# One gather in 48 of a two-layer graph kernel replaced by 128 single-row loads from SyncE and ScalarE

## The chip, the cores and the metric

The kernel runs on one core of one Trainium2 chip. The metric is device time in microseconds, from the first to the last instruction of one execution with what lies around it; lower is better. The kernel before took 4138.44 us, the median of three runs (4134.31 to 4139.52).

## The reference

Two rounds of message passing over a graph with 6250 nodes and 200000 edges (sorted by destination), 128 features each, all in float32. Cut to what matters:

```python
edge_index = jnp.stack([src, dst])
# layer 0
m = relu(concat([x[dst], x[src], edge_attr, u_edge]) @ W1.T + b1)
agg = segment_sum(m, dst, 6250)
x = layernorm(x + relu(concat([x, agg, u]) @ W2.T + b2))
# layer 1
h = relu(concat([x[src], x[dst], edge_attr]) @ msg_w1 + msg_b1)
agg = mean over incoming edges of (h @ msg_w2 + msg_b2)      # 0 where a node has none
x = layernorm(x + relu(concat([x, agg]) @ upd_w1 + upd_b1) @ upd_w2 + upd_b2)
```

## The kernel before

The product over a concatenation is split. Each layer first makes two tables in HBM with one row per node: `tabQ` (x times the weights of the source part, float32, 512 bytes a row) and `tabP` (the destination part with the bias, as three bfloat16 pieces). An edge's message is then relu(edge_attr·wc + tabP[dst] + tabQ[src]).

The program is a row of blocks, with all engines meeting between them: setup and tables of layer 0, `edges(0)`, `update(0)` (node update, layer norm, new `tabQ`), `between()` (new `tabP`), `edges(1)`, `update(1)`. The two `edges` blocks hold nearly all the time. Each works through NG = 391 groups of GE = 512 edges, a group being J = 4 tiles of P = 128 edges. For group g:

- SyncE (the queue SP) loads the edge attributes `ea` (1 MB for four groups, line 528, two buffers), the destination numbers `bc` (for eight groups, line 534) and, for every group, the 42 rows of `tabP` that can occur in it (`PB`, line 538). The address of these rows is read from SBUF into a register (`value_load`, line 537). Before it loads `PB` of group g, SyncE waits until TensorE has finished the products of group g-4 (line 536), so it works up to four groups ahead.
- GpSimd (POOL) gathers the `tabQ` rows of the 512 source nodes with four indirect DMAs of 128 rows (`gathers`, line 206) into a ring `Qr` of R_Q = 12 groups. For group g it waits until VectorE has used group g-12 (line 204). The first PF = R_Q - 2 = 10 groups are gathered ahead of the block: in layer 0 in the setup block (line 291), in layer 1 in `between()` (line 844).
- TensorE adds the edge product (line 615, eight passes for four float32 products) and the `tabP` part by a 0/1 matrix (line 619) into one of four PSUM banks, and raises `v_C`. The group's messages of two groups before are summed by destination with line 628 (and counted with line 631, layer 0 only).
- VectorE makes the 0/1 matrices (lines 570, 576, 582), adds the gathered rows to the PSUM bank (line 587, this raises `v_tt`), and adds a finished group's sums to the accumulator (line 598).
- ScalarE does nothing else in these blocks than wait for `v_tt` and apply the relu (line 557), which raises `v_rl` for TensorE.

Each engine runs its own list in order; what holds them together are these semaphores and the depths of the rings.

Of the kernel before, what the change touches and what calls it, by code (L numbers as in the profile page):

```python
# [12 lines left out]
N = 6250  # L13
# [22 lines left out]

R_EA, R_PB, R_BC, R_Q, R_ST, R_S, R_M, R_PT = 2, 4, 2, 12, 3, 6, 3, 4
LB = 8
R_C = 4
PF = R_Q - 2  # L40
NBIG = 11904

WALL = ("wq0", "wp0", "wc0", "wu0", "w2x", "w2a", "w2u", "wq1", "wp1", "wc1", "mwT", "uwx", "uwa", "uw2")
# [4 lines left out]
def build(nc, a, out):  # L48
    ctx = ExitStack()
    with ctx:  # L50
# [31 lines left out]
        Qr = sb("Qr", [P, R_Q * J * D])  # L82
        Q = Qr[:, :].rearrange("p (r j d) -> p r j d", r=R_Q, j=J)
        X = sb("X", [P, NB, D])
        XT = sb("XT", [P, NP])
# [42 lines left out]
        for l in range(2):  # L128
            v = {n: sems(f"{n}{l}_", r) for n, r in (("ea", 3), ("pb", R_PB), ("bc", R_BC), ("q", R_Q))}
            v.update((n, sem(f"{n}{l}")) for n in ("C", "st", "s", "cn", "tt", "rl", "A", "ag"))  # L130
            v.update((n, sem(f"{n}{l}")) for n in ("gg", "gsc"))
            es.append(v)
# [63 lines left out]
        def pieces_sync(e, l, p_lo):  # L196
            for c, (b, n) in enumerate(CH):
                e.wait_ge(p_lo, c + 1)
                e.dma_start(node_rows(tabP[l], c), P3[:, c % R_PT, 0:n, :]).then_inc(s_tabP[l][c % R_PT], 16)

        def gathers(e, l, g0, g1):
            for g in range(g0, g1):
                if g >= R_Q:
                    e.wait_ge(es[l]["tt"], g - R_Q + 1)
                for j in range(J):
                    e.indirect_dma_start(Q[:, g % R_Q, j, :], None, tabQ[l][:, :],  # L206
                                         bass.IndirectOffsetOnAxis(ap=srcE[:, g, j:j + 1], axis=0)).then_inc(es[l]["q"][g % R_Q], 16)

# [8 lines left out]
        RQB = 4  # L217
        VALID = E - (NG - 1) * GE
        VJ, VP = VALID // P, VALID % P

# [282 lines left out]
        def edges(l):  # L503
# [14 lines left out]
            with nc.Block() as block:  # L518
                @block.sync
                def _(e):  # L520
                    ok = e.value_load(flagI[0:1, 0:1], min_val=0, max_val=1)
                    with e.If(ok):
                        for g in range(NG):
                            if g % LQ == 0:
                                k = g // LQ
                                if k >= R_EA:
                                    e.wait_ge(v_C, LQ * (k - R_EA) + LQ)
                                e.dma_start(ea[:, k % R_EA, :], a["eaT"][k, :, :]).then_inc(v_ea[k % R_EA], 16)
                            if g % LB == 0:
                                k = g // LB  # L530
                                n = min(LB, NG - g)
                                if k >= R_BC:
                                    e.wait_ge(v_st, LB * (k - R_BC) + LB)
                                e.dma_start(bc[0:K, k % R_BC, 0:n * GE], a["dstR"][:, g * GE:(g + n) * GE].broadcast_to([K, n * GE])).then_inc(v_bc[k % R_BC], 16)
                            if g >= R_PB:
                                e.wait_ge(v_C, g - R_PB + 1)
                            base = e.value_load(baseI[0:1, g:g + 1], min_val=0, max_val=N - 1)
                            e.dma_start(PB[0:K, g % R_PB, :], tabP[l][bass.ds(base, W), :].rearrange("w (h d) -> (w h) d", d=D)).then_inc(v_pb[g % R_PB], 16)
                    with e.Else():
                        general_sync(e, l)  # L540
# [9 lines left out]
                @block.scalar  # L550
                def _(e):
                    ok = e.value_load(flagI[0:1, 0:1], min_val=0, max_val=1)
                    with e.If(ok):
                        for g in range(NG):
                            e.wait_ge(v_tt, g + 1)
                            m = M[:, g % R_M, :, :].rearrange("p j d -> p (j d)")
                            e.activation(m, m, ACT.Relu).then_inc(v_rl, 1)  # L557

                @block.vector
                def _(e):  # L560
                    ok = e.value_load(flagI[0:1, 0:1], min_val=0, max_val=1)
                    with e.If(ok):
                        for i in range(NG + 3):
# [14 lines left out]
                            if 0 <= g < NG:  # L578
# [4 lines left out]
                                e.wait_ge(v_C, g + 1)  # L583
                                e.wait_ge(v_q[g % R_Q], 64 * (g // R_Q + 1))
                                if g >= R_M:
                                    e.wait_ge(v_A, g - R_M + 1)
                                e.tensor_tensor(M[:, g % R_M, :, :].rearrange("p j d -> p (j d)"), bank[g % R_C][:, :],  # L587
                                                Q[:, g % R_Q, :, :].rearrange("p j d -> p (j d)"), ALU.add).then_inc(v_tt, 1)
                            if l == 1 and i % 16 == 15 and i // 16 < NC:
# [285 lines left out]
def laid_out(v):  # L875
    import numpy as _np

    def cut(m, b):
# [15 lines left out]
        "eaT": eap.reshape(NQ, LQ * GE, D).transpose(0, 2, 1),  # L894
        "srcL": srcp.astype(_np.int32).reshape(NGP, J, P).transpose(2, 0, 1).reshape(P, NGP * J),
        "dstL": dstp.astype(_np.int32).reshape(NGP, J, P).transpose(2, 0, 1).reshape(P, NGP * J),
        "dstR": dstp.astype(_np.int16).reshape(1, EP),
# [22 lines left out]
```

## Time and profile before

| | |
|---|---|
| runs | 4139.52, 4138.44, 4134.31 us |
| profiled execution | 4140.49 us, its span 4138.7 us |
| GpSimd busy | 2981.5 us (72%) |
| TensorE matmul busy | 3378.5 us (82%), granted clock 0.517 over the span |
| VectorE busy | 1671.5 us (40%) |
| ScalarE busy | 591.0 us (14%) |
| DMA | 569.11 MB, mean 138 GB/s |

An engine's busy time leaves out the time that its queue needs between two instructions, and for POOL it is the time to make the descriptors of a gather, not the time of the transfer. DMA issues on SyncE and ScalarE are not counted as busy; their durations are found in the rows of their line (SPq and ACTq are these two queues). Which engine bounds a block is read from who waits for whom in it.

### The profile page before, as it was taken

Reading aid. Unit: us, or ns where it says so; the run is one execution under the profiler, and the core shown is the slowest. Engines: PE = TensorE matmul, PEld = TensorE weight load, DVE = VectorE, ACT = ScalarE, POOL = GpSimd, SP = SyncE. Lnnn points to the kernel's source line nnn. Section 1 sums busy time; section 2 is a strip of 40 time slices with the busy share of each in tenths; the row PEclk is TensorE's granted clock in tenths of the full one; section 3 lists DMA queues with packets and bytes.
Section 4 is the critical chain, followed back from the end, with each engine's and each line's share of the span. In section 5 each row is a group of like instructions: output and inputs, shape, how many; then the busy total and the mean of one; then the engine's idle time right before and its main releaser. Section 6 shows DMA issues by size and latency. Waiting matters only on the chain. (4 is left out here: it accounts for less than half of the span.)

```text
span 4138.7 us, 53825 instructions
## 1 busy us (share of the span) xinstructions
PE 3378.5 (82%) x16906; PEld 3171.1 (77%) x16906; DVE 1671.5 (40%) x3965; ACT 591.0 (14%) x1005; POOL 2981.5 (72%) x3156
## 2 busy tenths in 40 slices
PE   6998788877888888788779878878788787887886
PEld 4998787777878778787759877777777777777773
DVE  4544444444444444444445443434333333333333
ACT  1111111111111111111321111111111111111113
POOL 4777777777777777777267777777777777777772
PEclk6555555555555555555755555555555555555556
DMA  6554444444444444444155444444444444444431
GB/s 227 167 162 130 140 131 145 143 133 140 131 140 142 139 140 131 140 135 143 53 159 172 140 142 140 131 139 130 140 143 138 140 131 140 132 148 141 131 118 34
DMA packets 286577, 569.11 MB, mean 138 GB/s; under 512 B 165416, under 2 KB 197523, under 8 KB 248976
## 3 DMA queue, kind: packets, MB, share of 16 engines
q1 hardware_dynamic: 185326, 357.82, 25.7%
q0 software_dynamic: 100096, 205.20, 18.6%
q8 instruction: 142, 2.33, 0.2%
q10 hardware_dynamic: 866, 2.56, 0.2%
q14 instruction: 147, 1.20, 0.1%
HBM read 545.86 MB, written 19.45 MB: 137 GB/s over the span
## 5 line engine op out<-in xcount | busy, mean ns | idle before, releaser
L206 POOL DMA_INDIRECT Qr<-tabQ,srcE x3128 | 2960.7, 947 | 1074.7 <-issue 969.1
L615 PE MATMUL bank<-wall,BIG 128*128 128x128 f32 x6256 | 1596.3, 436 | 35.0 <-DMA BIG<-in_eaT 35.0
L628 PE MATMUL bank<-BIG 128*128 128x42 f32 x6256 | 1459.8, 413 | 13.0 <-ACT BIG L557 13.0
L615 PEld LDWEIGHTS bank<-wall,BIG 128*128 128x128 f32 x6256 | 1419.2, 331 | 35.4 <-DMA BIG<-in_eaT 35.4
L628 PEld LDWEIGHTS bank<-BIG 128*128 128x128 f32 x6256 | 1420.7, 331 | 13.6 <-ACT BIG L557 13.6
L587 DVE TENSOR_TENSOR BIG<-bank,Qr 128x512 f32<-128x512 f32 x782 | 539.6, 690 | 2097.9 <-issue 1727.3
L619 PE MATMUL bank<-BIG 126*128 126x128 bf16 x3128 | 484.1, 310 | 648.4 <-DVE BIG L570 647.8
L557 ACT ACTIVATE BIG<-BIG 128x512 f32<-128x512 f32 x782 | 492.4, 630 | 3364.1 <-DVE BIG L587 3364.1
L619 PEld LDWEIGHTS bank<-BIG 126*128 126x128 bf16 x3128 | 339.3, 141 | 774.8 <-DVE BIG L570 748.1
L570 DVE TENSOR_TENSOR BIG<-bank,BIG 126x512 bf16<-126x512 f32 x782 | 534.2, 683 | 34.3 <-DMA BIG<-in_dstR 34.0
L576 DVE TENSOR_TENSOR BIG<-bank,relE 128x168 f32<-128x168 f32 x782 | 251.5, 322 | 0.0
L598 DVE TENSOR_TENSOR AC<-AC,bank 128x84 f32 (+1 forms) x782 | 171.0, 219 | 162.4 <-PE bank L631 40.4
L582 DVE TENSOR_REDUCE BIG<-BIG 128x42 bf16<-128x168 f32 x391 | 167.5, 428 | 0.0
L631 PEld LDWEIGHTS bank<-BIG,onesb 128*128 128x128 bf16 x391 | 113.1, 289 | 0.0
L631 PE MATMUL bank<-BIG,onesb 128*128 128x42 bf16 x391 | 93.6, 239 | 0.0
L164 PEld LDWEIGHTS bank<-wall,XT 128*128 128x128 f32 x196 | 42.9, 322 | 34.7 <-issue 34.7
L819 POOL TENSOR_SCALAR BIG<-AC 3x512 bf16<-3x512 f32 (+1 forms) x13 | 18.8, 1446 | 59.1 <-PE bank L704 49.8
L162 PE MATMUL bank<-c,ones 1*128 1x512 f32 (+1 forms) x52 | 48.8, 1036 | 5.0 <-PEq L664 3.4
L164 PE MATMUL bank<-wall,XT 128*128 128x128 f32 x196 | 50.5, 436 | 0.0
L190 DVE TENSOR_TENSOR bank<-bank,BIG 128x512 f32<-128x512 f32 (+1 forms) x26 | 17.4, 668 | 74.9 <-ACT BIG L180 74.9
L402 DVE RECIPROCAL AC<-AC 128x512 f32<-128x512 f32 (+1 forms) x13 | 41.0, 3156 | 0.0
L702 PE MATMUL bank<-BIG,mU 128*128 128x512 f32 (+1 forms) x26 | 20.1, 867 | 22.1 <-DVE BIG L733 22.1
(94 smaller groups left out, 481.0 us busy)
## 6 DMA issues: line engine op xcount, KB each, us to landing
BIG<-in_eaT SPq DMA_DIRECT2D x196, 1024.0 KB, 5.6
BIG<-in_dstR SPq DMA_DIRECT2D x96, 1008.0 KB
Qr<-tabQ,srcE POOLq DMA_INDIRECT x3128, 2.5
BIG<-tabP SPq DMA_DIRECT2D x782, 31.5 KB
tabP<-BIG SPq DMA_DIRECT2D x24, 384.0 KB, 2.8
tabQ<-BIG SPq DMA_DIRECT2D x24, 256.0 KB, 4.0
X<-in_xN SPq DMA_DIRECT2D x1, 3136.0 KB, 12.0
out<-BIG SPq DMA_DIRECT2D x12, 256.0 KB, 2.3
```

What stands on the lines that cost most here:

```text
L164: last = e.matmul(o[:, k * D:(k + 1) * D], XT[:, (b + k) * P:(b + k + 1) * P], wp[l], start=False, stop=(k == n - 1))
L206: e.indirect_dma_start(Q[:, g % R_Q, j, :], None, tabQ[l][:, :], bass.IndirectOffsetOnAxis(ap=srcE[:, g, j:j + 1], axis=0)).then_inc(es[l] ...
L557: e.activation(m, m, ACT.Relu).then_inc(v_rl, 1)
L570: e.tensor_tensor(ST[0:K, i % R_ST, :], bank[6][0:K, i:i + 1].broadcast_to([K, GE]), bc[0:K, k % R_BC, (i % LB) * GE:(i % LB + 1) * GE], A ...
L576: e.tensor_tensor(S[:, i % R_S, :, :], io, rel, ALU.is_equal).then_inc(v_s, 1)
L582: e.tensor_reduce(S16[:, g % R_S, :], S[:, g % R_S, :, :].rearrange("p j w -> p w j"), AX, ALU.add).then_inc(v_cn, 1)
L587: e.tensor_tensor(M[:, g % R_M, :, :].rearrange("p j d -> p (j d)"), bank[g % R_C][:, :], Q[:, g % R_Q, :, :].rearrange("p j d -> p (j d)" ...
L598: e.tensor_tensor(acc, acc, bank[4 + g % 2][:, 0:ctl * W].rearrange("p (t w) -> p t w", w=W), ALU.add).then_inc(v_ag, 1)
L615: e.matmul(bank[i % R_C][:, j * D:(j + 1) * D], ea[:, k % R_EA, (i % LQ * J + j) * P:(i % LQ * J + j + 1) * P], wc[l], start=(j == 0), sto ...
L619: last = e.matmul(bank[i % R_C][:, j * D:(j + 1) * D], ST[0:K, i % R_ST, j * P:(j + 1) * P], PB[0:K, i % R_PB, :], start=False, stop=(j == ...
L628: last = e.matmul(bank[4 + g % 2][:, 0:W], M[:, g % R_M, j, :], S[:, g % R_S, j, :], start=(j == 0), stop=(j == J - 1))
L631: last = e.matmul(bank[4 + g % 2][:, W:2 * W], onesb[:, :], S16[:, g % R_S, :], start=True, stop=True)
```

## The change

Every twelfth group from group 15 on (15, 27, ... 387: NH = 32 groups in each layer) is gathered with three indirect DMAs instead of four. The rows of its fourth tile are loaded one by one: 128 DMAs of one row of 512 bytes, each with its own address in a register, into a new buffer `Qx` (two slots of 128 rows). The row numbers come from a new small input `srcH`, one row of it per such group, loaded into `ixr` (one partition) by SyncE six groups ahead. The loads are spread over twelve groups: in each of them SyncE issues five (60 in all) after its `PB` load, and ScalarE six (68 in all, so the last group of the twelve has two) ahead of its relu. Each batch starts with one TENSOR_LOAD that fills its five or six registers. They are issued in groups 12h to 12h+11 for group 12h+15. VectorE adds such a group in two steps, 384 columns from the ring and then, after waits on the two queues' semaphores, 128 columns from `Qx`.

To make room for `Qx`, the ring `Qr` has R_Q = 11 groups instead of 12, and PF, which is R_Q - 2, goes from 10 to 9. The last group, which holds only 320 edges, is gathered with three indirect DMAs, the third of 64 rows, instead of four of 128.

```diff
@@ -34,11 +34,18 @@
 CH = [(b, min(4, NB - b)) for b in range(0, NB, 4)]
 NC = len(CH)
 
-R_EA, R_PB, R_BC, R_Q, R_ST, R_S, R_M, R_PT = 2, 4, 2, 12, 3, 6, 3, 4
+R_EA, R_PB, R_BC, R_Q, R_ST, R_S, R_M, R_PT = 2, 4, 2, 11, 3, 6, 3, 4
 LB = 8
 R_C = 4
 PF = R_Q - 2
 NBIG = 11904
+
+HP, HO = 12, 15
+ROWS_SP, ROWS_ACT = 5, 6
+NH = len(range(HO, NG - 1, HP))
+SPLIT = HP * ROWS_SP
+VALID = E - (NG - 1) * GE
+VJ, VP = VALID // P, VALID % P
 
 WALL = ("wq0", "wp0", "wc0", "wu0", "w2x", "w2a", "w2u", "wq1", "wp1", "wc1", "mwT", "uwx", "uwa", "uw2")
 WCOL = {n: i * D for i, n in enumerate(WALL)}
@@ -81,6 +88,8 @@
         K3 = sb("K3", [3, 5 * D], BF16)
         Qr = sb("Qr", [P, R_Q * J * D])
         Q = Qr[:, :].rearrange("p (r j d) -> p r j d", r=R_Q, j=J)
+        Qx = sb("Qx", [P, 2, D])
+        ixr = sb("ixr", [1, 2, P], I32)
         X = sb("X", [P, NB, D])
         XT = sb("XT", [P, NP])
         AC = sb("AC", [P, 2, NT])
@@ -128,7 +137,8 @@
         for l in range(2):
             v = {n: sems(f"{n}{l}_", r) for n, r in (("ea", 3), ("pb", R_PB), ("bc", R_BC), ("q", R_Q))}
             v.update((n, sem(f"{n}{l}")) for n in ("C", "st", "s", "cn", "tt", "rl", "A", "ag"))
-            v.update((n, sem(f"{n}{l}")) for n in ("gg", "gsc"))
+            v.update((n, sem(f"{n}{l}")) for n in ("gg", "gsc", "ix"))
+            v.update((n, sems(f"{n}{l}_", 2)) for n in ("rS", "rA"))
             es.append(v)
 
         gs = [{"ea": v["ea"][0], "all": v["ea"][1], "z": v["ea"][2], "g": v["gg"], "sc": v["gsc"],
@@ -198,13 +208,38 @@
                 e.wait_ge(p_lo, c + 1)
                 e.dma_start(node_rows(tabP[l], c), P3[:, c % R_PT, 0:n, :]).then_inc(s_tabP[l][c % R_PT], 16)
 
+        def by_rows(g):
+            return g >= HO and (g - HO) % HP == 0 and (g - HO) // HP < NH
+
+        def tiles(g):
+            return -(-VALID // P) if g == NG - 1 else J - by_rows(g)
+
+        def q_count(g):
+            return 16 * sum(tiles(i) for i in range(g % R_Q, g + 1, R_Q))
+
+        def row_loads(e, l, engine, s, g, n, lo, hi):
+            h, r = g // HP, g % HP
+            p0, p1 = lo + r * n, min(lo + (r + 1) * n, hi)
+            if h >= NH or p0 >= p1:
+                return
+            if r == 0:
+                e.wait_ge(es[l]["ix"], 16 * (h + 1))
+                if h >= 2:
+                    e.wait_ge(es[l]["tt"], (h - 2) * HP + HO + 1)
+            _, rows_at = nc.values_load_multi_w_load_instructions(
+                ixr[0:1, h % 2, p0:p1], engines=[engine], min_val=0, max_val=N - 1,
+                skip_runtime_bounds_check_because="an index of a node, which the gathers use as it is")
+            for p, at in zip(range(p0, p1), rows_at):
+                e.dma_start(Qx[p:p + 1, h % 2, :], tabQ[l][bass.ds(at, 1), :]).then_inc(s[h % 2], 16)
+
         def gathers(e, l, g0, g1):
             for g in range(g0, g1):
                 if g >= R_Q:
                     e.wait_ge(es[l]["tt"], g - R_Q + 1)
-                for j in range(J):
-                    e.indirect_dma_start(Q[:, g % R_Q, j, :], None, tabQ[l][:, :],
-                                         bass.IndirectOffsetOnAxis(ap=srcE[:, g, j:j + 1], axis=0)).then_inc(es[l]["q"][g % R_Q], 16)
+                for j in range(tiles(g)):
+                    p = VP if g == NG - 1 and j == VJ else P
+                    e.indirect_dma_start(Q[0:p, g % R_Q, j, :], None, tabQ[l][:, :],
+                                         bass.IndirectOffsetOnAxis(ap=srcE[0:p, g, j:j + 1], axis=0)).then_inc(es[l]["q"][g % R_Q], 16)
 
         s_id, s_idn, s_cst, s_wq, s_src, s_wl, s_row, s_dst, s_bas, s_cb, s_xn, s_z, s_zero = (
             sem(n) for n in ("s_id", "s_idn", "s_cst", "s_wq", "s_src", "s_wl", "s_row", "s_dst", "s_bas", "s_cb", "s_xn", "s_z", "s_zero"))
@@ -215,8 +250,6 @@
             sem(n) for n in ("s_v", "s_c0", "s_c1", "s_cd", "s_k", "s_kd", "s_flag", "s_vt"))
         p0 = [sem(f"p0_{n}") for n in ("c", "hi", "r", "mid", "lo")]
         RQB = 4
-        VALID = E - (NG - 1) * GE
-        VJ, VP = VALID // P, VALID % P
 
         def x_load(e, i):
             c0, c1 = XG[i]
@@ -520,6 +553,7 @@
                 def _(e):
                     ok = e.value_load(flagI[0:1, 0:1], min_val=0, max_val=1)
                     with e.If(ok):
+                        e.dma_start(ixr[0:1, 0, :], a["srcH"][0:1, :]).then_inc(v["ix"], 16)
                         for g in range(NG):
                             if g % LQ == 0:
                                 k = g // LQ
@@ -536,6 +570,12 @@
                                 e.wait_ge(v_C, g - R_PB + 1)
                             base = e.value_load(baseI[0:1, g:g + 1], min_val=0, max_val=N - 1)
                             e.dma_start(PB[0:K, g % R_PB, :], tabP[l][bass.ds(base, W), :].rearrange("w (h d) -> (w h) d", d=D)).then_inc(v_pb[g % R_PB], 16)
+                            row_loads(e, l, mybir.EngineType.SP, v["rS"], g, ROWS_SP, 0, SPLIT)
+                            h = g // HP + 1
+                            if g % HP == HP // 2 and h < NH:
+                                if h >= 2:
+                                    e.wait_ge(v_rl, (h - 1) * HP)
+                                e.dma_start(ixr[0:1, h % 2, :], a["srcH"][h:h + 1, :]).then_inc(v["ix"], 16)
                     with e.Else():
                         general_sync(e, l)
 
@@ -552,6 +592,7 @@
                     ok = e.value_load(flagI[0:1, 0:1], min_val=0, max_val=1)
                     with e.If(ok):
                         for g in range(NG):
+                            row_loads(e, l, mybir.EngineType.Activation, v["rA"], g, ROWS_ACT, SPLIT, P)
                             e.wait_ge(v_tt, g + 1)
                             m = M[:, g % R_M, :, :].rearrange("p j d -> p (j d)")
                             e.activation(m, m, ACT.Relu).then_inc(v_rl, 1)
@@ -581,11 +622,18 @@
                                     with nc.allow_low_precision(reason="a sum of four zeros or ones"):
                                         e.tensor_reduce(S16[:, g % R_S, :], S[:, g % R_S, :, :].rearrange("p j w -> p w j"), AX, ALU.add).then_inc(v_cn, 1)
                                 e.wait_ge(v_C, g + 1)
-                                e.wait_ge(v_q[g % R_Q], 64 * (g // R_Q + 1))
+                                e.wait_ge(v_q[g % R_Q], q_count(g))
                                 if g >= R_M:
                                     e.wait_ge(v_A, g - R_M + 1)
-                                e.tensor_tensor(M[:, g % R_M, :, :].rearrange("p j d -> p (j d)"), bank[g % R_C][:, :],
-                                                Q[:, g % R_Q, :, :].rearrange("p j d -> p (j d)"), ALU.add).then_inc(v_tt, 1)
+                                n = (J - by_rows(g)) * D
+                                m = M[:, g % R_M, :, :].rearrange("p j d -> p (j d)")
+                                last = e.tensor_tensor(m[:, 0:n], bank[g % R_C][:, 0:n], Qr[:, g % R_Q * J * D:g % R_Q * J * D + n], ALU.add)
+                                if by_rows(g):
+                                    h = (g - HO) // HP
+                                    e.wait_ge(v["rS"][h % 2], 16 * SPLIT * (h // 2 + 1))
+                                    e.wait_ge(v["rA"][h % 2], 16 * (P - SPLIT) * (h // 2 + 1))
+                                    last = e.tensor_tensor(m[:, n:], bank[g % R_C][:, n:], Qx[:, h % 2, :], ALU.add)
+                                last.then_inc(v_tt, 1)
                             if l == 1 and i % 16 == 15 and i // 16 < NC:
                                 last_terms(e, i // 16)
                             g = i - 3
@@ -893,6 +941,7 @@
         "xN": xp.reshape(NB, P, D).transpose(1, 0, 2).reshape(P, NB * D),
         "eaT": eap.reshape(NQ, LQ * GE, D).transpose(0, 2, 1),
         "srcL": srcp.astype(_np.int32).reshape(NGP, J, P).transpose(2, 0, 1).reshape(P, NGP * J),
+        "srcH": srcp.astype(_np.int32).reshape(NGP, J, P)[HO:HO + NH * HP:HP, J - 1, :],
         "dstL": dstp.astype(_np.int32).reshape(NGP, J, P).transpose(2, 0, 1).reshape(P, NGP * J),
         "dstR": dstp.astype(_np.int16).reshape(1, EP),
         "base": dstp.astype(_np.int32)[::GE].reshape(1, NGP),
```

What GpSimd's list holds around the start of `edges(0)` before (x40 are the gathers of the setup block, x1524 those of `edges(0)`):

```order
L287 AFFINE_SELECT third<-third 128x41
L206 DMA Qr<-tabQ,srcE 128x128 x40
L226 UNCONDITIONAL_BRANCH
L542 UNCONDITIONAL_BRANCH
L544 TENSOR_LOAD flagI
L544 ISA x2
L545 COMPARE_AND_BRANCH
L206 DMA Qr<-tabQ,srcE 128x128 x1524
```

And now:

```order
L320 AFFINE_SELECT third<-third 128x41
L241 DMA Qr<-tabQ,srcE 128x128 x36
L259 UNCONDITIONAL_BRANCH
L582 UNCONDITIONAL_BRANCH
L584 TENSOR_LOAD flagI
L584 ISA x2
L585 COMPARE_AND_BRANCH
L241 DMA Qr<-tabQ,srcE 128x128 x1494
L241 DMA Qr<-tabQ,srcE 64x128
```

Four gathers have left the setup block for the edge block, and the edge block holds 1495 instead of 1524; layer 1 is the same.

What SyncE does for one group before (L537 fetches the address of the `tabP` rows, L538 loads them):

```order
L537 TENSOR_LOAD baseI
L537 ISA x2
L538 ISA
L538 DMA BIG<-tabP 126x128
L537 TENSOR_LOAD baseI
```

And now, of which the last pair (L233) stands five times in a row before the next L571:

```order
L571 TENSOR_LOAD baseI
L571 ISA x2
L572 ISA
L572 DMA BIG<-tabP 126x128
L229 TENSOR_LOAD ixr
L233 ISA
L233 DMA Qx<-tabQ 1x128
```

Five DMAs of one row, with an address computation each and one register load ahead of them, now stand between two `tabP` loads.

ScalarE's list in an edge block before was one row:

```order
L552 ISA x2
L553 COMPARE_AND_BRANCH
L557 ACTIVATE BIG<-BIG 128x512 x391
L553 UNCONDITIONAL_BRANCH
L769 UNCONDITIONAL_BRANCH
```

And now the end of one batch of six (the pair L233 stands six times) and the start of the next, with the relu L598 between them:

```order
L229 TENSOR_LOAD ixr
L233 ISA
L233 DMA Qx<-tabQ 1x128
L233 ISA
L233 DMA Qx<-tabQ 1x128
L233 ISA
L233 DMA Qx<-tabQ 1x128
L233 ISA
L233 DMA Qx<-tabQ 1x128
L233 ISA
L233 DMA Qx<-tabQ 1x128
L233 ISA
L233 DMA Qx<-tabQ 1x128
L598 ACTIVATE BIG<-BIG 128x512
```

A relu now has six DMA issues of its own queue ahead of it.

## Rows read from the trace of the kernel before

**Rows 1.** The page's first part: busy us (share of the span) and instructions by engine.

```profile
PE 3378.5 (82%) x16906; PEld 3171.1 (77%) x16906; DVE 1671.5 (40%) x3965; ACT 591.0 (14%) x1005; POOL 2981.5 (72%) x3156
```

**Rows 2.** Waits by engine and line: us in total, times, longest.

```profile
DVE BIG L587 <- issue: 1727.3, 475, 8.7
POOL Qr L206 <- issue: 969.1, 3103, 15.7
...
DVE BIG L587 <- PE bank L619: 365.1, 194, 3.7
...
POOL Qr L206 <- DVE BIG L587: 9.3, 23, 1.6
```

**Rows 3.** L206 in `edges(0)`: us, POOL busy (x), granted clock, DMA share, GB/s.

```profile
104.00:1998.00 1894.00, 1431.56 (x1515) 0.50 0.46 139
```

**Rows 4.** Timeline of POOL, start of `edges(0)`: start us, us, line, [idle before].

```profile
76.90 0.94 POOL L206 DMA_INDIRECT Qr<-tabQ,srcE  x1 [0.30 <-issue]
93.55 0.94 POOL L206 DMA_INDIRECT Qr<-tabQ,srcE  x1 [15.71 <-issue]
...
104.86 0.94 POOL L206 DMA_INDIRECT Qr<-tabQ,srcE  x1 [1.62 <-DVE BIG L587]
```

**Rows 5.** Timeline of POOL, start of `edges(1)`.

```profile
2119.73 0.94 POOL L206 DMA_INDIRECT Qr<-tabQ,srcE  x1 [0.30 <-issue]
2129.01 0.94 POOL L206 DMA_INDIRECT Qr<-tabQ,srcE  x1 [8.33 <-issue]
```

**Rows 6.** Timeline, end of `edges(0)`: last gather and last use.

```profile
1998.18 0.94 POOL L206 DMA_INDIRECT Qr<-tabQ,srcE  x1 [0.30 <-issue]
...
2001.73 0.69 DVE L587 TENSOR_TENSOR BIG<-bank,Qr 128x512 f32<-128x512 f32 x1 [4.58 <-issue]
```

**Rows 7.** Timeline of TensorE, one group that nothing held up.

```profile
1002.20 2.06 PE L615 MATMUL bank<-wall,BIG 128*128 128x128 f32 x8
...
1006.22 0.56 PE L615 MATMUL bank<-wall,BIG 128*128 128x128 f32 x1
```

**Rows 8.** Instructions of L538 and L537: ns min/median/max, first and last start.

```profile
L538 SPq FUSED_REGOPS  x782: 42/42/48, 94.3 to 4012.8; - x196
L538 SPq MOVE BIG<-tabP x782: 29/29/38, 94.4 to 4012.9; - x196
L538 SPq DMA_DIRECT2D BIG<-tabP x782: 351/352/385, 94.4 to 4013.0; - x196
...
L537 SPq TENSOR_LOAD <-baseI x782: 427/432/539, 93.5 to 4012.1; - x196
```

**Rows 9.** Timeline of SP at 1019 us, and from 2129 us (four issues merged).

```profile
1019.33 0.35 SPq L538 DMA_DIRECT2D BIG<-tabP  x1
1019.72 0.37 SPq L528 DMA_DIRECT2D BIG<-in_eaT  x1
1020.13 0.41 SPq L534 DMA_DIRECT2D BIG<-in_dstR  x1
...
2130.36 4.41 SPq L538 DMA_DIRECT2D BIG<-tabP  x4
```

**Rows 10.** SyncE's own waits: us in total, times, longest.

```profile
SPq L537 <- PE bank L619: 2638.0, 770, 9.3
```

**Rows 11.** DMA issues of lines 239, 262, 249, 834 and 224, as in rows 8.

```profile
L239 SPq DMA_DIRECT2D baseI<-in_base x1: 333/333/333, 23.9 to 23.9; - x1
...
L262 ACTq DMA_DIRECT2D rows<-in_rows x1: 583/583/583, 3.6 to 3.6; - x1
...
L249 SPq DMA_DIRECT2D K<-BIG x3: 576/589/644, 88.2 to 89.5; - x3
...
L834 SPq DMA_DIRECT2D out<-BIG x1: 273/273/273, 4135.8 to 4135.8; - x1
...
L224 SPq DMA_DIRECT2D XT<-in_xT x4: 414/430/871, 0.8 to 2.2; - x4
L224 ACTq DMA_DIRECT2D XT<-in_xT x3: 446/454/709, 1.2 to 2.2; - x3
```

## The prediction

> **What bounds the kernel now.** I read the busy times first, then who waits for whom, then single stretches of the timeline. The page names TensorE as the busiest engine, 82% against 72% for POOL [rows 1]. The waits say otherwise. VectorE's addition of the gathered rows (L587) waits 1727.3 us in 475 cases for "issue", which is time in which no instruction of another engine releases it, and only 365.1 us for TensorE [rows 2]. POOL, which fills those rows, hardly ever waits for a buffer: 9.3 us in 23 cases; its other idle time, 969.1 us in 3103 cases, is again "issue", the 0.30 us that its queue needs between two gathers [rows 2, 4]. So POOL issues without a pause. The rate: 1515 gathers in 1894 us, 1.250 us each, whatever else goes on [rows 3]; that is 5.00 us for a group of four. TensorE, where nothing holds it up, does a group in 1006.22 - 1002.20 = 4.02 us [rows 7], in the layer that has the most to do. It is busy at both ends of a wait for POOL. At the end of `edges(0)` the last gather's descriptors are done at 1999.12 and the last addition starts at 2001.73, 2.6 us later [rows 6]: the transfer's latency, and no backlog behind it. Both edge blocks are as long as POOL's list.
>
> **What POOL saves.** In each layer 32 groups lose one gather of four, and the last group loses one: 33 gathers. But PF falls from 10 to 9, and the prefetch lies in time that POOL has free: in layer 0 it ends at 77.84 and the edge block's first gather starts at 93.55, in layer 1 at 2120.67 and 2129.01 [rows 4, 5]. One group fewer there is one group more in the block. So the block has 33 - 4 = 29 gathers fewer, 29 x 1.250 = 36.25 us a layer, 72.5 us in both. At the block's start nothing else moves: before, POOL gathers groups 10 and 11 freely and for group 12 waits for the first addition, until 104.86, 1.3 us more than its usual gap [rows 4]; now it gathers groups 9 and 10 and waits for the same addition with group 11. The last gather has 64 rows instead of 128. No row shows how its 0.94 us scales; between nothing and half of it saved, I take 0.3 us a layer. Against that SyncE issues one more DMA (`ixr`) ahead of the first `ea` load, some 0.4 us a layer [rows 9], which delays the first addition and with it POOL. Together: 72.5 + 0.6 - 0.8 = 72.3 us. VectorE gets one more instruction and two waits in one group of twelve, some 0.3 us in 59, and is busy 40% of the time [rows 1]; nothing.
>
> **What SyncE must now do, and whether it can.** This is where the change can fail. Let X be the time for which the issue of a single-row DMA holds its queue. Around it stand an address computation and a move, 42 + 29 ns [rows 8], and a gap of 0.04 us before each of the three (1019.72 + 0.37 to 1020.13 [rows 9]): X + 0.19 us a row. A `PB` load with its register load takes 1.35 us when SyncE does four in a row ((4.41 - 0.35) / 3 [rows 9]). `ea` and `bc`, 0.41 us in four groups and 0.45 in eight, add 0.16; the `ixr` load 0.03 in twelve. The register load ahead of five rows is one instruction; for one value it is 0.43 us [rows 8], and with a gap and the slowing that it shows behind a DMA 0.56. Per group SyncE then needs 1.35 + 0.16 + 0.03 + 0.56 + 5 x (X + 0.19) = 3.05 + 5X us. Before, it had 2638.0 / 782 = 3.4 us of every group free [rows 10].
>
> When does this bound the block? SyncE has no head start, as POOL has nine groups. Its first `PB` load is issued at 94.4 [rows 8], now 94.8; with a period p that of group 384, the first one free of row loads, is issued at 94.8 + 384p. It lands about 2.6 us later; the products of that group (0.6), six more groups at TensorE's own 4.02 (24.1) and the last addition (1.0) put the end at 123.1 + 384p. POOL alone ends at 2001.7 - 36.2 = 1965.5, so SyncE takes over at p = 4.80, X = 0.35, and the gain is gone at 123.1 + 384p = 2001.7: p = 4.89, X = 0.37. From p = 4.80 on the time is 4138.4 + 768 x (p - 4.89).
>
> X itself is not in the trace of before, and the nearest rows lie on both sides. The shortest issue of the profile took 0.273 us, 106 rows on their way out [L834, rows 11]. The one DMA that is most like a row load, one partition, one piece, from HBM, issued by SyncE, took 0.333 us [L239, rows 11]. `PB`, also with its address in a register but 126 rows, took 0.352 [rows 8]. Two others of one partition took longer: 0.583 on ScalarE, right behind the load of the weights, and 0.576 to 0.644 from SBUF to SBUF [rows 11]. I take 0.333: same engine, same route, same shape. Then p = 4.72, under 4.80 by 0.08, and POOL's list stays the bound. The ends for X are 0.273 and 0.583; by the lower one p = 4.42 and nothing changes, since POOL is the bound; by the upper one p = 5.97 and the time is 4138 + 768 x 1.08 = 4967 us. So the whole forecast hangs on 20 ns of an issue.
>
> ScalarE has more room: 68 rows in twelve groups, 68 x 0.523 + 12 x (0.56 + 0.1) = 43.5 us or 3.6 us a group. A relu has its six issues ahead of it in the queue, but these start when the relu before is dispatched, so they are done before the next addition comes, 4.9 us later on average; where two additions come closer a relu is late by tenths of a microsecond, and TensorE, which needs it two groups later, has 4.90 - 4.02 = 0.9 us to spare in each group.
>
> The row loads of a group are issued by group 12h+11 and read in 12h+15, three groups (14 us) later at least, against a landing of about 2.6 us. The bytes are the same as before.
>
> **A rule that speaks against it.** Where both queues issued at once, at 0.8 to 2.2 us, an issue took 0.43 us on SyncE and 0.45 on ScalarE in the median, against 0.35 to 0.37 for loads of the same 128 rows later, with SyncE alone [rows 9, 11]. The Trainium skill, "Perfetto Trace Analysis", section "DMA Instruction — HWDGE (DVE, Sync)", says that the block which generates descriptors is shared by the two issuing sequencers and locked for exclusive use, and that the recorded time includes the wait for the lock. By that rule the rows are explained, and the 0.333 us above, measured with ScalarE silent, is too low. If the lock were held as long for one row as for 128, the time would be that of the second rival's upper end. Against it I set that with X + 0.19 = 0.52 us between two issues of a queue both fit beside each other, where the start of the program had 0.04 us between them.
>
> **The rivals.**
> - SyncE just over: X between 0.35 and 0.37, p between 4.80 and 4.89. Part of the gain is left, 4070 to 4130 us. For it: `PB`'s own 0.352. Chance 0.09, and 0.04 that it lands within 8 us of before.
> - SyncE well over, slower than before: the two queues hold each other up. By the rows of the program's start X is 0.43 at full overlap, p = 5.20, 4376 us; ScalarE issues in 3.6 of 4.9 us and collides in part of these, so X = 0.39, p = 5.00, 4138.4 + 768 x 0.11 = 4223 us is its middle. It decides from X = 0.37. For it: rows 11, L224. Against it: the free time between issues, and that a one-row DMA has one descriptor to make and not 128. Chance 0.18.
> - One-partition issues are dear, 0.583 us: 4967 us. For it: three of the four kinds in rows 11 that are slow are of one partition; against it L239. Then ScalarE too needs (68 x 0.773 + 7.9) / 12 = 5.0 us a group. Chance 0.03.
> - The change doesn't do what it says, since the rows land late: with one row in 0.42 us over both queues and each on the same path, VectorE would wait at its second addition in one group of twelve. Nothing in the rows shows it; 2 us in each of 64 groups would bring no loss as long as the ring has eleven groups of slack. Only a rate under one row in 0.46 us (59 us / 128) bounds, and a loss by that has chance 0.04.
>
> **How the numbers follow.** POOL stays the bound: 0.62. The profiled execution took 4140.5 us, 2.1 more than the median of the runs; less 72.3 it is 4068.2, and against the median 4138.4 - 72.3 = 4066 us. This is the forecast; its own range is 4060 to 4071 (the last gather's half, the start of the blocks). A measurement can tell about 0.2% from no change, 8 us. Faster: 0.62 + 0.09 = 0.71; within 0.2%: 0.04; slower: 0.18 + 0.03 + 0.04 = 0.25. The range for all cases must take in part of the second rival: 4058 to 4215 leaves out some 0.02 below and 0.16 above.
>
> **What would show it.** Right: 1495 gathers in each edge block, still 1.25 us apart, with SyncE waiting for TensorE some 0.1 to 0.3 us in each group on average, where it was 3.4; row-load issues of 0.33 us; POOL's waits for VectorE still under 20 us. Wrong: issues of 0.37 us and more, SyncE's waits gone, TensorE waiting for `PB` and POOL waiting for VectorE with a full ring. If the second addition (the 128 columns) shows waits for DMA, the rows land late. If gathers take longer than 1.25 us apart, the row loads disturb POOL and the sum's first term is wrong.

## The result, and the profile after

The changed kernel takes 4179.96 us (median of 4 runs, 4177.46 to 4183.31), the kernel before beside it 4137.50 (4 runs, 4134.31 to 4139.52): the ratio is 1.0104 [1.0086, 1.0121]. It is slower by 42 us, where 72 us less than before, 4066 us, was forecast. It lies in the range for all cases (4058 to 4215), on the slower side, which had a chance of 0.25.

The busy times of the kernel after show what the change was meant to take away: POOL has 67 us and 66 instructions less than in [rows 1].

```profile
PE 3387.9 (81%) x16906; PEld 3207.8 (77%) x16906; DVE 1669.1 (40%) x4029; ACT 591.0 (14%) x1005; POOL 2914.3 (70%) x3090
```

Its waits, in the columns of [rows 2] (L630 is the addition that was L587, L241 the gathers, L663 the products with the edge features, L611 the first use of a group's `bc`):

```profile
ACT BIG L598 <- issue: 1715.1, 533, 4.0
...
DVE BIG L611 <- DMA BIG<-in_dstR: 1050.4, 98, 15.7
POOL Qr L241 <- issue: 944.9, 2983, 19.1
DVE BIG L630 <- PE bank L667: 624.9, 571, 7.1
...
PE bank L663 <- DMA BIG<-in_eaT: 464.4, 181, 21.4
...
POOL Qr L241 <- DVE BIG L630: 61.4, 72, 5.0
...
DVE BIG L630 <- issue: 22.6, 14, 4.6
```

The largest wait of [rows 2] is gone. Before, the addition stood 1727.3 us for "issue", which was POOL's pace; now that is 22.6 us, and in its place TensorE waits for `ea`, VectorE for `bc` and the addition for TensorE. (For `PB` itself TensorE waits 19.6 us in 9 cases.) Both loads come from SyncE, and `ea` takes no longer to arrive than before (5.2 us from issue to landing in the median, before 5.6). They are issued late, since SyncE has hardly a wait left in which it could have issued them earlier. Its own waits say so, where [rows 10] had 2638.0 us in 770 cases:

```profile
SPq L571 <- PE bank L667: 38.3, 64, 2.8
```

SyncE now waits for a finished product in 64 of 782 groups and goes on at once in the 718 others. It has next to no free time, and its queue is the bound of both edge blocks. POOL is ahead of it: it waits for the addition 61.4 us with a full ring. Its rate has not changed (L241 in the first edge block, columns as in [rows 3]): 1470 gathers in 1854 us are 1.261 us each with those waits in them, and next to each other they start 1.25 us apart.

```profile
106.00:1960.00 1854.00, 1386.48 (x1470) 0.50 0.45 140
```

What fills SyncE's queue is seen in two lines of code: the load of a batch of numbers into registers (L229) and the row loads (L233). Columns as in [rows 8]:

```profile
L229 ACTq TENSOR_LOAD <-ixr x768: 667/1013/1802, 93.5 to 4042.8; - x192
L229 SPq TENSOR_LOAD <-ixr x768: 685/1287/1493, 94.9 to 4040.9; - x192
...
L233 ACTq DMA_DIRECT2D Qx<-tabQ x4352: 224/231/665, 94.7 to 4044.4; - x198
...
L233 SPq DMA_DIRECT2D Qx<-tabQ x3840: 224/233/283, 95.8 to 4044.1; - x192
```

The issue of a row load is cheap, 0.233 us where 0.333 was taken. The register load ahead of the rows is not: five numbers take 1.287 us in the median and 0.685 at least, against the 0.56 of the sum. One cycle of SyncE in its timeline (start, duration):

```profile
1003.83 1.93 SPq L233 DMA_DIRECT2D Qx<-tabQ  x5
...
1006.80 0.36 SPq L572 DMA_DIRECT2D BIG<-tabP  x1
...
1008.68 1.92 SPq L233 DMA_DIRECT2D Qx<-tabQ  x5
```

The five rows take 1.93 us, so one follows the other by (1.93 - 0.23) / 4 = 0.42 us. Between the end of the `PB` issue and the first row load lie 1008.68 - 1007.16 = 1.52 us, and 1.31 of it is one register load. At another group the same stretch is 2152.07 - 2151.11 = 0.96 us:

```profile
2150.72 0.39 SPq L572 DMA_DIRECT2D BIG<-tabP  x1
2152.07 1.93 SPq L233 DMA_DIRECT2D Qx<-tabQ  x5
```

That is group 0, whose five numbers start at byte 0 of the list. The instructions are the same in the two cycles. Of the twelve batches of SyncE, each 20 bytes long and right behind the one before, those at byte 0, 80 and 160 take 0.69 to 0.75 us in the median of 64 each. The nine others, none of which starts at a multiple of 16, take 1.29 to 1.31 us, those at a multiple of 8 (40, 120 and 200) too. The mean is 1.16 us. (Bytes are counted from the start of a slot of `ixr`.)

**Where the time lies.** The last additions of the two blocks after:

```profile
2019.40 0.69 DVE L630 TENSOR_TENSOR BIG<-bank,Qr 128x512 f32<-128x512 f32 x1 [1.62 <-PE bank L667]
...
4077.00 0.69 DVE L630 TENSOR_TENSOR BIG<-bank,Qr 128x512 f32<-128x512 f32 x1 [1.97 <-PE bank L667]
```

and the last one of the second block before:

```profile
4040.73 0.69 DVE L587 TENSOR_TENSOR BIG<-bank,Qr 128x512 f32<-128x512 f32 x1 [4.91 <-DMA Qr<-tabQ,srcE]
```

The last addition of the first block comes at 2019.40, before at 2001.73 [rows 6]: 17.7 us. The first `PB` load of the second block comes at 2150.72, before at 2130.36, which is 2.7 us more. From there to the last addition (4077.00, before 4040.73) it takes 15.9 us more. Together these are 36.3 of the 37.0 us by which the spans of the two profiled executions differ (4175.7 and 4138.7). The medians of the runs differ by 42.5: the profiled execution after (4177.46 us) was the fastest of its four, and the one before (4140.49 us) took longer than each of the four beside it.

### The profile page after: what moved, and what is told of

It reads as the page before. It is cut to its first block and busy times, and to the rows that moved or that the text cites. A ratio compares the mean times of both kernels' runs of the same rounds, so it can differ in the third digit from the quotient of the medians.

```text
span 4175.7 us, 80185 instructions
## 1 busy us (share of the span) xinstructions
PE 3387.9 (81%) x16906; PEld 3207.8 (77%) x16906; DVE 1669.1 (40%) x4029; ACT 591.0 (14%) x1005; POOL 2914.3 (70%) x3090
## 3 DMA queue, kind: packets, MB, share of 16 engines
q0 software_dynamic: 97984, 200.80, 17.9%
## 5 line engine op out<-in xcount | busy, mean ns | idle before, releaser
L241 POOL DMA_INDIRECT Qr<-tabQ,srcE x3062 | 2893.5, 945 | 1143.8 <-issue 944.9
L663 PE MATMUL bank<-wall,BIG 128*128 128x128 f32 x6256 | 1608.8, 439 | 464.6 <-DMA BIG<-in_eaT 464.4
L663 PEld LDWEIGHTS bank<-wall,BIG 128*128 128x128 f32 x6256 | 1418.7, 332 | 493.6 <-DMA BIG<-in_eaT 493.4
L676 PE MATMUL bank<-BIG 128*128 128x42 f32 x6256 | 1465.5, 414 | 0.0
L676 PEld LDWEIGHTS bank<-BIG 128*128 128x128 f32 x6256 | 1427.0, 333 | 0.0
L598 ACT ACTIVATE BIG<-BIG 128x512 f32<-128x512 f32 x782 | 492.4, 630 | 3398.4 <-issue 1715.1
L611 DVE TENSOR_TENSOR BIG<-bank,BIG 126x512 bf16<-126x512 f32 x782 | 535.8, 685 | 1050.8 <-DMA BIG<-in_dstR 1050.4
L630 DVE TENSOR_TENSOR BIG<-bank,Qr 128x512 f32<-128x512 f32 (+1 forms) x782 | 530.3, 678 | 647.5 <-PE bank L667 624.9
L667 PEld LDWEIGHTS bank<-BIG 126*128 126x128 bf16 x3128 | 385.2, 148 | 331.6 <-DVE BIG L611 273.4
```

The source lines that it names most:

```text
L241: e.indirect_dma_start(Q[0:p, g % R_Q, j, :], None, tabQ[l][:, :], bass.IndirectOffsetOnAxis(ap=srcE[0:p, g, j:j + 1], axis=0)).then_inc(e ...
L611: e.tensor_tensor(ST[0:K, i % R_ST, :], bank[6][0:K, i:i + 1].broadcast_to([K, GE]), bc[0:K, k % R_BC, (i % LB) * GE:(i % LB + 1) * GE], A ...
L630: last = e.tensor_tensor(m[:, 0:n], bank[g % R_C][:, 0:n], Qr[:, g % R_Q * J * D:g % R_Q * J * D + n], ALU.add)
L663: e.matmul(bank[i % R_C][:, j * D:(j + 1) * D], ea[:, k % R_EA, (i % LQ * J + j) * P:(i % LQ * J + j + 1) * P], wc[l], start=(j == 0), sto ...
L667: last = e.matmul(bank[i % R_C][:, j * D:(j + 1) * D], ST[0:K, i % R_ST, j * P:(j + 1) * P], PB[0:K, i % R_PB, :], start=False, stop=(j == ...
L676: last = e.matmul(bank[4 + g % 2][:, 0:W], M[:, g % R_M, j, :], S[:, g % R_S, j, :], start=(j == 0), stop=(j == J - 1))
```

## The experiments

Theory 1 says that SyncE's queue is the bound, and that what overfills it is the register load wherever its numbers don't start at a multiple of 16 bytes. Its rivals: the two queues hold each other up (the prediction's second rival), and the shorter ring, which fell from 12 to 11 groups to make room for `Qx`, costs the time.

**Numbers aligned (e1), and all of them off by four bytes (e2).** Each batch gets a slot of eight numbers of its own in `ixr`, in both kernels; the loads, rows and queues stay as in the kernel after. The second has SHIFT = 1.

```
+SLOT, SHIFT = 8, 0
...
+            at0 = SHIFT + (r + (HP if lo else 0)) * SLOT
...
-                ixr[0:1, h % 2, p0:p1], engines=[engine], min_val=0, max_val=N - 1,
+                ixr[0:1, h % 2, at0:at0 + p1 - p0], engines=[engine], min_val=0, max_val=N - 1,
```

> The changed kernel with one thing moved: each batch of row numbers (five for SyncE, six for ScalarE) starts at a multiple of 32 bytes in ixr, so that every register load reads from an aligned address; the counts of loads, gathers and waits stay. Theory 1 (SyncE's list is too long because its register load of five numbers takes 1.29 us where it starts off a multiple of 16 bytes and 0.69 to 0.75 where it starts on one): all SyncE register loads 0.69 to 0.75 us, SyncE's period per group falls from 4.93 to about 4.49 us, POOL's list is the bound again, 4066 to 4074 us. Theory 2 (SyncE and ScalarE hold each other up in the DMA issues, or the sheer number of issues bounds): the register loads stay as they are or the time that they save comes back as longer issues, 4160 to 4190 us.

> The same layout, but each batch starts 4 bytes behind a multiple of 32 bytes, so that no register load is aligned. Theory 1: the three SyncE loads of twelve that were aligned go from 0.73 to 1.29 us, the period of SyncE rises by 0.14 us to 5.07, the time by 768 x 0.14 = 107 us to about 4287 us; ScalarE's loads are all 1.59 us without effect on the time. Theory 2: nothing depends on the address, 4180 us.

Measured: 4069.51 us (5 runs, 4065.60 to 4072.96), ratio to before 0.9831 [0.9817, 0.9844]; and 4277.79 us (4 runs, 4275.09 to 4283.57), 1.0335 [1.0319, 1.0350]. With the same work, the same number of instructions and the same bytes of rows, e2 takes 208 us longer than e1, by where a batch of five or six numbers begins. The register loads of e1 (L232 here) and SyncE's wait for its condition:

```profile
L232 ACTq TENSOR_LOAD <-ixr x768: 661/936/1184, 93.9 to 3931.5; - x192
L232 SPq TENSOR_LOAD <-ixr x768: 674/737/915, 95.3 to 3908.5; - x192
```

```profile
SPq L574 <- PE bank L670: 222.2, 125, 6.9
```

and of e2:

```profile
L232 ACTq TENSOR_LOAD <-ixr x768: 657/1579/1840, 93.8 to 4141.8; - x192
L232 SPq TENSOR_LOAD <-ixr x768: 1225/1288/1485, 95.2 to 4138.0; - x192
```

```profile
SPq L574 <- PE bank L670: 42.0, 77, 2.8
```

The median for SyncE is 0.737 us in one and 1.288 in the other, and in the kernel after it is a mixture of the two. In e1 POOL is the bound again: the addition waits for "issue" 1300.5 us, POOL for the addition only 20.9:

```profile
DVE BIG L633 <- issue: 1300.5, 380, 8.3
...
POOL Qr L244 <- DVE BIG L633: 20.9, 44, 3.8
```

SyncE's period, from the first `PB` load of a block to that of group 384, is 4.74 us in e1, 4.93 in the kernel after and 5.06 in e2. From after to e2 three more batches of twelve are slow, which by (1.288 - 0.73) x 3 / 12 should add 0.14 us; measured is 0.13.

**ScalarE's row loads left out (e3).** ScalarE issues none, its 68 rows of `Qx` stay zero, and the second addition doesn't wait for them (POOL sets `Qx` to zero once, in the setup). SyncE's part is untouched.

```
                         for g in range(NG):
-                            row_loads(e, l, mybir.EngineType.Activation, v["rA"], g, ROWS_ACT, SPLIT, P)
...
-                                    e.wait_ge(v["rA"][h % 2], 16 * (P - SPLIT) * (h // 2 + 1))
```

> The changed kernel without ScalarE's row loads (68 rows of Qx stay zero, so that part of the sums is left out); SyncE's five loads per group stay. Theory 1: SyncE's list is as long as before, only its first issue of a batch loses some hundredths of a microsecond, period 4.87 to 4.93 us, 4130 to 4180 us, register loads of 1.29 us as before. Theory 2 (the two queues hold each other up): SyncE's period falls under 4.80 and the time to 4066 to 4075 us.

Measured: 4170.79 us (4 runs, 4167.30 to 4173.73), 1.0076 [1.0061, 1.0092]. Without 4352 of the 8192 row loads and their register loads the kernel is still slower than before. SyncE's issues have the same median, and its wait is as small:

```profile
L233 SPq DMA_DIRECT2D Qx<-tabQ x3840: 224/233/283, 96.2 to 4033.2; - x192
```

```profile
SPq L572 <- PE bank L666: 35.4, 60, 2.8
```

Its period is 4.919 us against 4.934, so ScalarE's queue costs SyncE's some 0.015 us a group, 12 us of the time at most. The rival of the two queues has the sign right and a fraction of the size.

**All gathers kept, row loads added (e5).** POOL saves nothing: `tiles(g)` is J for every group, and the rows are still loaded and added.

```
         def tiles(g):
-            return -(-VALID // P) if g == NG - 1 else J - by_rows(g)
+            return J
...
-                    p = VP if g == NG - 1 and j == VJ else P
+                    p = P
```

> The changed kernel with all four gathers of every group left in (the last group's too) and the row loads beside them: the change's cost without its gain. Theory 1 (SyncE's list bounds, so the dropped gathers gain nothing): the same time as the changed kernel, 4180 us (4172 to 4188). Rival (POOL's list bounds still, and something in the row loads slows it): by POOL's gathers the time would rise by 29 + 4 gathers of 1.25 us a layer over the changed kernel, to about 4260 us; by POOL alone without the row loads it would be 4150 us.

Measured: 4183.07 us (4 runs, 4180.39 to 4185.32), 1.0107 [1.0091, 1.0122], against 1.0104 of the kernel after. The 66 gathers that the change saves are worth nothing that can be told, and what makes the kernel slower comes with the loads (the ring is 11 groups long here as in e1, which is fast). POOL waits for the addition 32.4 us instead of 61.4; that is where part of its saving went, into standing with a full ring:

```profile
POOL Qr L241 <- DVE BIG L630: 32.4, 64, 5.2
```

**The kernel before with a ring of 11 (e4), and with the whole ring prefetched (e6).**

```
-R_EA, R_PB, R_BC, R_Q, R_ST, R_S, R_M, R_PT = 2, 4, 2, 12, 3, 6, 3, 4
+R_EA, R_PB, R_BC, R_Q, R_ST, R_S, R_M, R_PT = 2, 4, 2, 11, 3, 6, 3, 4
```

and in e6 also

```
-PF = R_Q - 2
+PF = R_Q
```

> The kernel before with a ring of 11 groups (PF 9), nothing else. Theory 1: POOL fills the ring and stands still until the first addition in each edge block, so it has one group less done at that moment, 4 x 1.25 = 5.0 us a layer, 10 us in all: 4148 us. Rival: the ring is deeper than the work needs, 4138 us.

> The kernel before with a ring of 11 groups and all 11 groups gathered ahead of the edge blocks (PF 11 instead of 9). Theory 1 (what costs is the ring: POOL stands still with a full ring until the first addition, whatever was gathered ahead): as the ring of 11 with PF 9, 4150 us, at best 2 us a layer less since the block's first loads have the DMA engines to themselves, 4146 to 4150. The prediction's reading (the cost is the group that leaves the free time of the setup block): the loss is gone, 4138 us or less.

Measured: 4150.19 us (10 runs), 1.0024 [1.0015, 1.0034]; and 4146.96 us (11 runs), 1.0018 [1.0009, 1.0027]. A ring of 11 costs 10 us, 7 with the whole of it prefetched. The intervals overlap: how many groups are prefetched makes no difference that can be told, how many the ring holds does. The timeline of POOL at the start of the first block shows why, in e4

```profile
93.27 0.94 POOL L206 DMA_INDIRECT Qr<-tabQ,srcE  x1 [20.34 <-issue]
...
106.72 0.94 POOL L206 DMA_INDIRECT Qr<-tabQ,srcE  x1 [3.76 <-DVE BIG L587]
```

and in e6:

```profile
106.31 0.94 POOL L206 DMA_INDIRECT Qr<-tabQ,srcE  x1 [23.56 <-DVE BIG L587]
```

POOL stands with a full ring until the first addition in both. What counts is how many groups it has by then, and that is the ring. No run has `Qx` beside a ring of 12.

**Other splits of the rows, aligned (e7, e8).** Both start from e1. In e7 one gather in 40 is replaced, with 5 rows a group by SyncE and 8 by ScalarE, and the whole ring is prefetched; in e8 it is 4 and 7, one gather in 48.

```
-HP, HO = 12, 15
-ROWS_SP, ROWS_ACT = 5, 6
+HP, HO = 10, 13
+ROWS_SP, ROWS_ACT = 5, 8
...
-PF = R_Q - 2
+PF = R_Q
```

```
-ROWS_SP, ROWS_ACT = 5, 6
+ROWS_SP, ROWS_ACT = 4, 7
```

> Aligned register loads, one gather in 40 instead of 48 replaced (every tenth group from group 13 on, 38 groups a layer; SyncE five rows a group, ScalarE eight), and all 11 groups of the ring gathered ahead. Theory 1: POOL's list loses 6 more gathers a layer, 15 us, and stays the bound: 4048 to 4056 us. SyncE's own time per group is unchanged at about 4.5 us, ScalarE's 8 x 0.39 + 0.9 = 4.0. Rival: ScalarE's queue now delays the relu so that TensorE waits for it, 4070 us or more.

> Aligned register loads with four rows a group on SyncE and seven on ScalarE (48 + 80). Theory 1: the time is POOL's, 4066 to 4073 us, since SyncE was no longer the bound. If an aligned group of four numbers is fetched as one, SyncE's register load takes as long as that of one number, 0.43 to 0.55 us, and ScalarE's of seven 0.25 us more than its one of six; if each number costs 0.06 us, SyncE's takes 0.68 us.

Measured: 4051.62 us (5 runs, 4048.73 to 4055.34), 0.9793 [0.9779, 0.9806], the fastest of all; and 4065.82 us (one run, so its time stands without an interval). Six more gathers saved in each layer are 12 x 1.25 = 15 us, and e7 is 17.9 under e1. It also differs from e1 by the prefetch of the whole ring, which made 3 us between e4 and e6, no more than can be told there. The loads of e7:

```profile
L232 ACTq TENSOR_LOAD <-ixr x760: 562/794/1296, 93.6 to 3892.8; - x190
L232 SPq TENSOR_LOAD <-ixr x760: 673/739/952, 95.0 to 3874.2; - x190
```

and of e8, with SyncE's wait:

```profile
L232 ACTq TENSOR_LOAD <-ixr x768: 877/1207/1425, 93.6 to 3929.2; - x192
L232 SPq TENSOR_LOAD <-ixr x768: 457/522/772, 95.1 to 3906.8; - x192
```

```profile
SPq L574 <- PE bank L670: 746.9, 499, 7.2
```

SyncE has 525 us more to spare in e8 than in e1, and the time is the same within a run's spread (e1's own runs go from 4065.60 to 4072.96). So in e1 POOL was the bound, as the first term of the prediction has it.

## Why the prediction was wrong

**What bounded the kernel before, and what POOL saves: right.** Where SyncE is kept under its limit, in e1, the kernel takes 4069.51 us against a forecast of 4066, in the likeliest case's own range of 4060 to 4071. One part of the working was wrong and right in its sum: the head start that is lost belongs to the ring (e4, e6), not to the prefetch. POOL waits for the first addition with a full ring whatever was prefetched. One group less in the ring is four gathers in each block, 10 us, as the sum had it and as e4 measured (7 in e6). Some 3 of these may be the first addition, which in e4 and e6, as in the kernel after, frees POOL 1.5 to 1.9 us later than in [rows 4]; why is open.

**The row loads' issue, X: too dear.** The prediction took 0.333 us from the one issue that looked most alike (L239 in [rows 11]) and put 0.273 as the lower end. Measured: 0.233, under both. The 0.19 us around each issue was right: the spacing of 0.42 us is 0.233 + 0.19.

**The register load: the step that failed.** The prediction said "The register load ahead of five rows is one instruction; for one value it is 0.43 us [rows 8], and with a gap and the slowing that it shows behind a DMA 0.56". It took the price of one number for five, gave it no upper end, and so left it out of the range. By the timeline above the stretch from the `PB` issue to the first row load is 1.52 us in nine groups of twelve and 0.96 in three, 1.38 in the mean, where the sum had 0.56 for the load and 0.19 for what stands ahead of the first row, 0.75. That is 0.63 us a group too little. By the prediction's own terms: 3.05 + 5 x 0.233 = 4.22; with 0.63 for the register load, 0.05 for the `PB` step (1006.80 + 0.36 - 1005.76 = 1.40 instead of 1.35) and 0.05 for what SyncE still waits (38.3 / 782) it is 4.95, and measured were 4.93. The two errors had opposite signs: with the true X alone the period would have been 4.2 us and the forecast safe.

The prediction did not weigh a figure for this. The Trainium skill, "Runtime: NRT & Kernel Launch", section "Instruction fetch mechanics", says of the register loads that the runtime adds that they cost about 200 ns for each register even in bulk. An estimate by that page of the Trainium skill is 5 x 0.2 = 1.0 us for SyncE's batch. Where the numbers don't start at a multiple of 16 bytes the traces show 0.3 to 0.4 us more than that (1.29 us for five, 1.58 for six); where they do, eight numbers took 0.79 us, half of it.

**From the period to the time: right in form, 8 us short.** With 4.934 us, the mean of the two blocks, the prediction's formula gives 4138.4 + 768 x 0.044 = 4172 us; measured are 4180. From the `PB` load of group 384 to the last addition the prediction had 28.3 us; it is 2019.40 - 1988.33 = 31.1 and 4077.00 - 4046.16 = 30.8. The second block also starts 2.7 us later. The rows at the end of the second block, of SyncE and VectorE:

```profile
4044.75 0.40 SPq L568 DMA_DIRECT2D BIG<-in_dstR  x1
4046.16 4.77 SPq L572 DMA_DIRECT2D BIG<-tabP  x4
...
4051.93 0.69 DVE L611 TENSOR_TENSOR BIG<-bank,BIG 126x512 bf16<-126x512 f32 x1 [9.53 <-DMA BIG<-in_dstR]
```

Group 384 is a multiple of eight, so its `ea` and `bc` are issued just ahead of its `PB`, and the `bc` is there 7.2 us after its issue. The prediction had only the `PB` load's 2.6 us. From 4051.93 to the last addition the seven groups follow at TensorE's own pace, and POOL has long been done:

```profile
4039.16 0.90 POOL L241 DMA_INDIRECT Qr<-tabQ,srcE  x1 [0.30 <-issue]
```

Its last gather starts 38 us before the last addition, where in [rows 6] it was 3.6. That backlog is the plainest sign in the trace that POOL no longer bounds. The 0.90 us are those of a gather of 64 rows: half the rows save 0.04 us and not 0.3.

**The rivals.** The second had the place and the sign right, and no run contradicts its deciding point: SyncE is the bound, and at periods of 4.93 and 5.06 us, above the 4.89 of the prediction, the kernel is slower than before. Its cause was wrong. It has an X of 0.37 and more by the two queues holding each other up; X is 0.233 and e3 leaves 0.015 us a group for the other queue. The rule that the prediction weighed there, of the block that makes descriptors and is locked ("Perfetto Trace Analysis", section "DMA Instruction — HWDGE (DVE, Sync)" of the Trainium skill), is not contradicted: an issue of 0.23 us in 0.42 leaves room for the other queue's. It costs next to nothing here, 0.015 us a group at most. The longest single-row issue was 0.283 us on SyncE and 0.665 on ScalarE. The third rival, dear issues of one partition, is out by the same rows; so is the fourth, since the second addition (L635) has no idle time before it in any of its 64 cases.

**ScalarE: the need was in reach, the delay larger than told.** The prediction had relus late "by tenths of a microsecond". In 533 groups the relu comes after an idle time that "issue" ends, 3.2 us in the mean: its turn in the queue came after the row loads. By the starts of L598 and the ends of its additions the relu is 2.0 us late in the median, where it was 0.03 before, and over 1 us late in 535 of 782 groups. It costs nothing, since the product that reads it (L676) has no idle time before it. But the reason given for it, that the row loads are done before the addition comes, holds in a quarter of the groups: in 186 the relu starts within 0.3 us.

## What to carry to other kernels

An engine that issues DMAs from registers must be costed as an engine: all of its instructions for one step of the loop, with the register load priced by how many numbers it takes and where they begin. An instruction whose size the profile before does not show gets an upper end of its own, above all where its neighbour in the sum gets all the attention; here the whole care went into X, and the time hung on the term beside it. Where the addresses come from a table in SBUF, lay each batch at a multiple of 16 bytes.

## What the runs showed of the hardware

A register load from SBUF is priced by the number of its values and by whether it starts at a multiple of 16 bytes. Medians of the rows above: four numbers in one aligned group take 0.52 us, five 0.74, six 0.94, seven 1.21 and eight, two full groups, 0.79 (the last three on ScalarE); off the alignment five take 1.29 and six 1.58. One number alone took 0.43 us in [rows 8], and 0.52 in the kernel after, behind other issues:

```profile
L571 SPq TENSOR_LOAD <-baseI x782: 434/524/748, 93.5 to 4061.2; - x196
```

So in a load that starts at a multiple of 16 bytes a full group of four costs about what one number does, and each number beyond it 0.2 to 0.27 us more. In a load that starts elsewhere each further number costs some 0.2 us, and a full aligned group inside it saves nothing: in the kernel after, SyncE's batches at byte 60, 140 and 220 hold one from their second number on, and take 1.29 us like the others. A multiple of 32 isn't needed (byte 80: 0.75 us). Two numbers, ScalarE's last batch of twelve, take 0.74 us in e1 and e2 alike. What the queue does inside was not measured.

The issue of a one-row DMA with its address in a register holds the queue for 0.23 us, against 0.36 for the 126 rows of `PB`, and rows can follow each other by 0.42 us on SyncE.
